# Mixture-of-experts blocks that scatter their rows into token order, instead of a gather afterwards

## The reference

```python
# e0: 8 experts, hidden 704; e1: 7 experts, hidden 256, plus a shared expert; e3: 8 experts, hidden 512
probs = router(x)                       # softmax, or sigmoid in e1
w, idx = top_k(probs, 2); w = w / sum(w)
for each token t and k in (0, 1):
    e = idx[t, k]
    y[t] += w[t, k] * (silu(x[t] @ gate[e]) * (x[t] @ up[e])) @ down[e]
```

## Time and profile before

| | |
|---|---|
| span of the profiled execution | 2167.4 us |
| median of three runs | 2168.05 us |
| TensorE busy | 1686.6 us (78%) |
| VectorE busy | 1150.7 us (53%) |
| ScalarE busy | 544.3 us (25%) |
| GpSimd busy | 544.7 us (25%) |
| HBM read / written | 231.86 MB / 30.02 MB |
| mean granted TensorE clock | 0.891 of full speed |

### The profile page before, as it was taken

One profiled execution on the slowest core, in us unless ns is written; L12 is line 12 of the kernel. 1 busy time (PEld: TensorE's weight loads), 2 busy tenths in 40 slices (PEclk: granted clock), 3 DMA queues, 4 the chain that ended last, 5 costly groups with the idle time before them and its releaser, 6 DMA issues. The chain is left out here.

```text
span 2167.4 us, 36689 instructions
## 1 busy us (share of the span) xinstructions
PE 1686.6 (78%) x10302; PEld 1354.6 (62%) x10302; DVE 1150.7 (53%) x2756; ACT 544.3 (25%) x1372; POOL 544.7 (25%) x812
## 2 busy tenths in 40 slices
PE   3994999997269787999994878716799599499990
PEld 2772889886169644666663467605566487398980
DVE  5774222221966667777767223365788577422223
ACT  1441011010134223556551110002222254110100
POOL 1001111111510014666652033250122100222215
PEclk8996999999589888999997899955899799699995
DMA  3103889986200026535301078830000000399983
GB/s 111 35 0 114 293 295 304 299 288 222 75 1 0 0 73 121 74 42 73 43 1 39 15 236 267 250 94 1 0 0 0 1 0 0 127 324 313 322 272 119
DMA packets 182133, 262.59 MB, mean 121 GB/s; under 512 B 17504, under 2 KB 132640, under 8 KB 180032
## 3 DMA queue, kind: packets, MB, share of 16 engines
q1 hardware_dynamic: 171856, 234.01, 36.2%
q0 software_dynamic: 10224, 27.93, 4.8%
HBM read 231.86 MB, written 30.02 MB: 121 GB/s over the span
## 5 line engine op out<-in xcount | busy, mean ns | idle before, releaser
L992 POOL TENSOR_TENSOR l1a_pr<-l1a_pr,l1a_rc (+4 forms) x256 | 176.0, 719 | 113.5 <-DVE l1a_rc L932 113.4
L956 ACT ACTIVATE l1a_pr<-l1a_sc,l1a_nm 128x256 f32 (+7 forms) x256 | 131.4, 525 | 113.3 <-DVE l1a_nm L926 113.3
L1049 PE MATMUL l1a_ob<-l1a_pT,xn 128*128 128x512 f32 (+3 forms) x512 | 148.5, 434 | 0.0
L1049 PEld LDWEIGHTS l1a_ob<-l1a_pT,xn 128*128 128x128 f32 x512 | 92.3, 191 | 50.9 <-issue 30.6
L1578 PEld LDWEIGHTS e0b_gp<-e0b_xT,e0b_wgu 128*128 128x128 f32 x936 | 109.4, 195 | 14.7 <-issue 12.3
L1162 POOL DMA_INDIRECT e_got<-y_slots,e_slot x96 | 99.8, 1040 | 73.7 <-issue 71.4
L1578 PE MATMUL e0b_gp<-e0b_xT,e0b_wgu 128*128 128x128 f32 x936 | 116.9, 283 | 1.8 <-DVE e0b_hT L1647 1.3
L1599 PE MATMUL e0b_yp<-e0b_wd,e0b_hT 128*128 128x256 f32 x468 | 115.2, 388 | 0.6 <-issue 0.6
L926 DVE TENSOR_REDUCE l1a_nm<-l1a_sc 128x1 f32<-128x512 f32 (+3 forms) x256 | 107.2, 482 | 0.2 <-PE l1a_sc L1027 0.2
L1628 ACT ACTIVATE e0b_sg<-e0b_gp 128x640 f32<-128x640 f32 x78 | 33.5, 481 | 288.0 <-PE e0b_gp L1578 288.0
L519 PE MATMUL a_sc<-a_kd,a_qT 128*128 (+2 forms) x256 | 99.4, 523 | 4.4 <-ACT a_qT L592 2.9
(11 more groups left out here) (475 smaller groups left out, 3581.3 us busy)
## 6 DMA issues: line engine op xcount, KB each, us to landing
e3b_wgu<-in_L_ffn_W SPq DMA_DIRECT2D x78, 512.0 KB, 5.6
e0b_wgu<-in_L_ffn_gate_proj SPq DMA_DIRECT2D x39, 704.0 KB, 4.6
e0b_wgu<-in_L_ffn_up_proj SPq DMA_DIRECT2D x39, 704.0 KB, 6.0
e0b_wd<-in_L_ffn_down_proj SPq DMA_DIRECT2D x39, 640.0 KB, 5.2
e3b_wd<-in_L_ffn_W SPq DMA_DIRECT2D x39, 512.0 KB, 6.4
e1b_wgu<-in_L_ffn_Wg_r SPq DMA_DIRECT2D x39, 256.0 KB, 3.8
e1b_wgu<-in_L_ffn_Wu_r SPq DMA_DIRECT2D x39, 256.0 KB, 4.5
e1b_wd<-in_L_ffn_Wd_r SPq DMA_DIRECT2D x39, 256.0 KB, 4.0
```

What stands on the lines that cost most here:

```text
L956: nc.scalar.activation(pr[:, n & 1, of_query[q]], sc[q][:, 0:(q + 1) * P], ACT.Exp, bias=nm[:, q:q + 1], accum_out=sums[:, n & 1, q:q + 1] ...
L992: nc.gpsimd.tensor_tensor(of, of, bcast(rc[:, n & 1, q:q + 1], 2, (q + 1) * P), ALU.mult)\
L1049: last = nc.tensor.matmul(ob[:, k * P:], vz[:, k, h * P:(h + 1) * P], pT[:, n & 1, key_at[k]:key_at[k] + TB - k, :], start=(h == 0 and k = ...
```

## The change

- The blocks' results are no longer stored by SP. POOL stores them: `send(n, j)` waits until `copy_out(n)` is done, copies a column of the new table `target` into `row`, waits for it, runs a filler and issues an indirect DMA (a scatter) from `yb` into `y_rows`, whose row number is 256 + 2048 k + token. Places without a token write into the first 256 rows. `send(n)` stands at the end of POOL's `step(n)`, behind the fetch of block n+3 and in front of the `step(n+1)` that fetches block n+4.
- `route` makes `target` beside `token`: seven VectorE instructions at its end instead of three. Two constants grow or are added.
- In the combination, POOL issues nothing more. SP issues eight plain loads of four token tiles each (128 x 4 rows of 1 KB, 512 KB), alternately for k = 0 and 1, into a ring of four. Load n of 4 or later waits until the tiles of load n-4 are used. In e0 and e1 they stand behind `beside.load` in SP's queue.

```diff
+    y_rows = nc.dram_tensor("y_rows", [2 * P + TOP * B * S, D], F32, kind="Internal").ap()
+    RING, RING_TILES = 4, 4
...
-                        for n in range(T * TOP):
-                            if n >= RING:
-                                pool.wait_ge(used, n - RING + 1)
-                            pool.indirect_dma_start(got[:, n % RING, :], None, y_slots[0:NB * P, :], bass.IndirectOffsetOnAxis(
-                                ap=slot[n % TOP][:, n // TOP:n // TOP + 1], axis=0)).then_inc(rows_got[n % RING], 16)
...
+                        for n in range(LOADS):
+                            if n >= RING:
+                                sp.wait_ge(used, (n - RING) // TOP * TOP * RING_TILES + (RING_TILES - 1) * TOP + n % TOP + 1)
+                            c, k = n // TOP, n % TOP
+                            sp.dma_start(got[:, n % RING, :, :], by_token[k, :, c * RING_TILES:(c + 1) * RING_TILES, :])\
+                                .then_inc(rows_got[n % RING], 16)
...
-                    nc.vector.tensor_copy(token_p[:], found[:, 1, :]).then_inc(step, 1)
+                    nc.vector.tensor_scalar(token_p[:], found[:, 1, :], float(B * S - 2 * P), None, ALU.add).then_inc(step, 1)
+                    nc.vector.scalar_tensor_tensor(spare_row[:], found[:, 0, :], 0.0, const("spare"), ALU.is_equal, ALU.mult)\
+                        .then_inc(step, 1)
...
-                    dve.wait_ge(step, 32)
-                    nc.vector.tensor_copy(token[:], token_f[:])
+                    dve.wait_ge(step, 33)
+                    nc.vector.tensor_copy(token_i[:], token_f[:]).then_inc(step, 1)
+                    nc.vector.scalar_tensor_tensor(target_f[:], token_f[:], float(2 * P - B * S), spare_row[:], ALU.add, ALU.add)\
+                        .then_inc(step, 1)
+                    dve.wait_ge(step, 34)
+                    nc.vector.tensor_scalar(token[:], token_i[:], B * S - 1, None, ALU.bitwise_and)
+                    dve.wait_ge(step, 35)
+                    nc.vector.tensor_copy(target[:], target_f[:])
...
-                        if positive(n):
-                            store(n - 1, 1 - j)
-
-                    def store(n, j):
-                        sp.wait_ge(y_copied, n + 2)
-                        sp.dma_start(y_slots.rearrange("(n p) d -> n p d", p=P)[n], yb[j][:]).then_inc(rows_out[j], 16)
...
+                    def send(n, j):
+                        pool.wait_ge(y_copied, n + 2)
+                        nc.gpsimd.tensor_copy(row[j][:], target[:, bass.ds(n, 1)]).then_inc(row_ready, 1)
+                        pool.wait_ge(row_ready, n + 1)
+                        nc.gpsimd.tensor_tensor(spare[:], const("place"), const("place"), ALU.add)
+                        pool.indirect_dma_start(y_rows, bass.IndirectOffsetOnAxis(ap=row[j][:], axis=0), yb[j][:], None)\
+                            .then_inc(rows_out[j], 16)
...
                         fetch(1 - j)
+                        send(n, j)
...
+                    send(0, 0)
                     with pool.Fori(0, (NB - 5) // 2) as i:
                         for j in (1, 0):
                             step(i * 2 + 2 - j, j)
                     step(NB - 4, 1)
+                    for n in (NB - 3, NB - 2, NB - 1):
+                        send(n, n % 2)
```

More of the change, by code:

```diff
@@ L61, in _constants @@
         "iota128": np.tile(np.arange(P), (P, 1)),
-        "tiles": np.tile(np.arange(T), (P, 1)),
+        "tiles": np.tile(np.arange(TOP * T) + 2, (P, 1)),
+        "spare": p[:, None] + P * (np.arange(ROUTED)[None, :] % 2),
         "place": p[:, None],
@@ L142, in build @@
     x_rows = nc.dram_tensor("x_rows", [B * S, D], F32, kind="Internal").ap()
-    y_slots = nc.dram_tensor("y_slots", [SLOTS, D], F32, kind="Internal").ap()
-    RING = 16
+    y_rows = nc.dram_tensor("y_rows", [2 * P + TOP * B * S, D], F32, kind="Internal").ap()
+    RING, RING_TILES = 4, 4
     pool_sem = lambda n: ctx.enter_context(nc.semaphore(n))
@@ L1128, in experts @@
             token = tmp("token", [P, ROUTED], U32)
+            target = tmp("target", [P, ROUTED], U32)
             with ExitStack() as s2:
@@ L1131, in experts @@
                 normalise(f"{tag}n", x, xn, rms_weight, (lp, wr, E), st6)
-                route(tag, lp, E, wt, slot, owner, token, bias, x, outer)
+                route(tag, lp, E, wt, slot, owner, token, target, bias, x, outer)
             if shared:
                 shared_expert(f"{tag}s", *shared, F, into)
-            blocks(tag, w_gate, w_up, w_down, F, NB, E, owner, token)
+            blocks(tag, w_gate, w_up, w_down, F, NB, E, owner, token, target)
             with ExitStack() as s2:
                 sem = Semaphores(nc, s2, tag)
-                got = s2.enter_context(nc.sbuf_tensor(f"{tag}_got", [P, RING, D], F32))
+                got = s2.enter_context(nc.sbuf_tensor(f"{tag}_got", [P, RING, RING_TILES, D], F32))
                 used = sem("used")
+                LOADS = T * TOP // RING_TILES
+                by_token = y_rows[2 * P:].rearrange("(k t p) d -> k p t d", k=TOP, p=P)
                 if beside is not None:
@@ L1175, in _ @@
                                 beside.round(dve, n // 8)
-                            dve.wait_ge(rows_got[n % RING], 16 * (layer * T * TOP // RING + n // RING + 1))
+                            load = t // RING_TILES * TOP + k
+                            dve.wait_ge(rows_got[load % RING], 16 * (layer * LOADS // RING + load // RING + 1))
                             if n:
                                 dve.wait_ge(used, n)
-                            nc.vector.scalar_tensor_tensor(into[:, t, :], got[:, n % RING, :], wt[k][:, t:t + 1], into[:, t, :],
-                                                           ALU.mult, ALU.add).then_inc(used, 1)
+                            nc.vector.scalar_tensor_tensor(into[:, t, :], got[:, load % RING, t % RING_TILES, :], wt[k][:, t:t + 1],
+                                                           into[:, t, :], ALU.mult, ALU.add).then_inc(used, 1)
                             if k == TOP - 1 and t:
@@ L1274, in _, with route @@
                     add(B - 1)
-    def route(tag, lp, E, wt, slot, owner, token, bias, x, outer):
+    def route(tag, lp, E, wt, slot, owner, token, target, bias, x, outer):
         NB = ROUTED
@@ L1302, in route @@
             token_p, token_f = tmp("token_p", [P, ROUTED]), tmp("token_f", [P, ROUTED])
+            token_i, spare_row, target_f = tmp("token_i", [P, ROUTED], U32), tmp("spare_row", [P, ROUTED]), tmp("target_f", [P, ROUTED])
             found = ps("found", [P, 2, ROUTED])
@@ L1337, in _ @@
                     for k in range(TOP):
-                        nc.gpsimd.tensor_tensor(numbers[k][:, :, 0, :], at_hot[k][:], bcast(const("tiles"), 2, ROUTED), ALU.mult)\
+                        nc.gpsimd.tensor_tensor(numbers[k][:, :, 0, :], at_hot[k][:],
+                                                bcast(const("tiles")[:, k * T:(k + 1) * T], 2, ROUTED), ALU.mult)\
                             .then_inc(hot, 1)
@@ L1446, in _, with blocks @@
                         .then_inc(step, 1)
-                    dve.wait_ge(step, 32)
-                    nc.vector.tensor_copy(token[:], token_f[:])
-    def blocks(tag, w_gate, w_up, w_down, F, NB, experts_n, owner, token):
+                    dve.wait_ge(step, 33)
[6 more added lines that the diff above has]
+                    nc.vector.tensor_copy(target[:], target_f[:])
+    def blocks(tag, w_gate, w_up, w_down, F, NB, experts_n, owner, token, target):
         assert F % P in (0, P // 2)
@@ L1477, in blocks @@
             index = [st.enter_context(nc.sbuf_tensor(f"{tag}b_index{j}", [P, 1], U32)) for j in range(2)]
+            row = [st.enter_context(nc.sbuf_tensor(f"{tag}b_row{j}", [P, 1], U32)) for j in range(2)]
             spare = tmp("spare", [P, 1])
-            index_ready = sem("index")
+            index_ready, row_ready = sem("index"), sem("row")
             gu_in, d_in = ([sem(f"{n}{j}") for j in range(2)] for n in ("guin", "din"))
@@ L1531, in _ @@
                     step(NB - 2, 1, gate_up=False)
-                    for n in (NB - 2, NB - 1):
-                        store(n, n % 2)
                     sp.wait_ge(rows_out[0], 16 * (before[0] + NB // 2 + 1))
```

## The result

The kernel after takes 2222.09 us (median, 2220.1 to 2226.64), the kernel before 2168.41 us on the same chip: a ratio of 1.0244, 95% interval 1.0224 to 1.0265. It is slower, and by more than was forecast: the median lies 43 us above the 2179, and 15 us above the upper end of the range. The profiled execution has a span of 2219.1 us, 51.7 more than before, and a mean granted TensorE clock of 0.881 (before 0.891).

The account below looks back on a forecast made before the run. Bound: e3's combination by POOL's gathers, the blocks by TensorE, in e1 partly by weight loads. Combination -22.2, route +2.1, POOL's order +19.4 in e1 and +11.8 in e3 sum to +11.1 us on 2168.05: 2179, range 2155 to 2207.

Parts of the forecast that it names:

- The loop: Blocks: copy-out, send, fetch, landing, turn, up, down, copy-out over two blocks; costs +19.4 us in e1, +11.8 in e3, 0 in e0.
- first piece: Blocks, from the copy's end to the fetch's DMA: notice 0.17, send 0.75 + 0.99, index copy 0.75, together 2.66 us.
- The landing L in e1: Time from the fetch's DMA start to its landing in e1's blocks: between 2.9 and 4.4 us, taken as 3.4.
- The upper bound: e1's blocks: landing of 4.4 us, giving 4.93 us a block, +1.06, and up to +37 us.
- the last piece, turn to copy: Blocks, from the turn's start to the copy's end: 2.69 us in e1, 4.45 in e3.
- 5.45 + L: Length of e1's closed loop over two blocks, L being the fetch's landing; with 3.4 it is 8.85 us, 4.43 a block.
- The way out of the blocks: Each stage's end, last copy to SP's next load: notice and issue 0.92, landing 2.9, then 0.37: 4.2 us against 2.1.
- Combination and route: Combination: e3 -16.5, e1 -7.8, e0 +2.1, together -22.2 us; route: four more VectorE instructions a stage, +2.1 us for three.
- The fast landing: Rival, blocks: stall thins out the traffic, fetches land fast; e1 costs 11 us, e3 little or nothing; 2159, chance 0.25.
- the queue behind the send: Rival, blocks: fetch queues behind the send in the one software queue, landing 5.6 in e3, 4.4 in e1; 2209, chance 0.13.
- The case that the eight loads don't keep up: Rival, combination: a pair lands after 7.5 us instead of 4.9, the ring stalls twice a stage; +12 us, 2191, chance 0.07.
- list of signs: Periods 4.4 in e1, 6.0 in e3; some 35 turns wait; index copy follows send; e3's combination about 29 us, additions 0.655 apart.

Follow-up runs that it names:

- e0: Not a run: one of the kernel's three expert stages, hidden size 704; its block period is 7.99 us in both the kernel before and after.
- e3: Not a run: the expert stage that ends last, hidden size 512; its block period is 5.74 us in the kernel before, 5.97 after.
- fetch_first: Kernel after, with POOL's send of block n-1 behind the fetch of block n+3, one block later than in the change: 2159.68 us, ratio to before 0.9931.
- wait_and_filler: Kernel before with SP's stores; POOL's step also waits for the same copy-out, copies a column and runs a 1.04 us filler, no scatter: 2217.11 us.
- last_by_sp: Kernel after, but SP stores blocks 37 and 38 of each stage with plain DMAs to the spare rows: 2202.57 us, ratio to before 1.0146.
- half_weights: Kernel after, but e1's gate and up loads bring half of their bytes from block 2 on: 2199.69 us.
- merged: fetch_first with the combination in the expert blocks' block of programs, no barrier between, matrices loaded ahead of SP's wait: 2125.86 us, ratio to before 0.9792.

## Why the prediction was wrong, and where it was right

The direction and the mechanism were right, and two terms of the sum were too small: e1's blocks by 31 us and the ways out of the blocks by 12. Both errors point the same way, and together they carry the result out of the range.

*The loop.* It exists as described: its first piece was forecast at 2.66 and is 2.62, e3's period at 6.06 and is 5.97 (pieces 2.55, 4.91 and 4.48 us), e0's loss at nothing and it is nothing. For e1, fetch_first and wait_and_filler show it from both sides. For e3 only fetch_first does: with the loop opened e3's loss is gone, but wait_and_filler, whose loop is 0.55 us shorter, shows no loss there. (The base of 3.87 us a block was read off the stores; the copies give 3.92, which changes little.)

*The landing L in e1.* The step that failed is "L falls as the stall grows; I take 3.4". I had taken it for a function of the average DMA share. The share fell indeed, further than thought (0.65), and still fetch to turn is 4.28 us over the turns that waited, where the forecast had 3.5. These traces say that what is issued beside the fetch counts more. In the iteration shown above SP's loads of gate and up (1353.80 and 1354.37) are issued right ahead of the fetch at 1354.71, whose turn waits. The next fetch, at 1357.96, comes 3.6 us behind them and 3.5 ahead of the next two, and its turn doesn't wait. The trace of after has no landings of the indirect DMAs. That of last_by_sp has them, with the same blocks up to 36: 4.1 us on average for the fetches whose turn waits, 2.9 for the others. half_weights shows that the bytes of those loads cost 0.9 us. The upper bound, the measured median of 4.4, was the better value.

*TensorE's clock.* Missing from the sum altogether, and the larger of the two errors. I carried the last piece, turn to copy, over from the trace of before at 2.69, where TensorE had no long idle time and a clock of 0.98. The added stall was taken as spread over all blocks, half a microsecond each. It comes bunched instead: 18 waits of 3.0 us, one for every two blocks, and behind 15 of them the piece takes over 3.3 us, up to 4.67, with the granted clock at its lower level for a part or all of it. The step is the last term of "5.45 + L": 4.06 behind a turn that waited, instead of 2.69, and 2.76 behind one that didn't. Of the 2.00 us by which the waiting loop is longer than forecast (10.85 for 8.85), 1.37 are this piece and 0.78 the landing, while the first piece gives 0.15 back. By a rule in the Trainium skill ("TensorE: Matmul & The Clock Gate", section "HAM oscillation — how this bites in real kernels"), a kernel whose short stretches of matmuls alternate with waits for DMA is thrown back to the half clock over and over. This case's trace agrees: 0.82 in e1, and 0.98 again with dummy work in the waits. The two errors feed each other, since a longer wait lets the clock fall and the slower products lengthen the loop: a block takes 5.25 us with both, 4.64 with TensorE kept busy, 4.57 with half of the gate and up traffic; the forecast, with neither, was 4.43. Why the waits pair up isn't settled; POOL issues send, fetch, send, fetch in a row behind one copy-out (1353.07 to 1357.96), which would do it.

*The way out of the blocks.* The step that failed is "Sum 0.92 + 2.9 + 0.37 = 4.2". The landing in it was fine, even a little high: merged measures 3.14 from the last copy to the first load. But the 0.37 came from a stage whose last instructions were SP's stores, while POOL had issued its last indirect DMA 14 us earlier. What isn't in that row is POOL's drain ahead of the barrier, 6.44 us from the end of its last indirect DMA. 0.67 to the scatter, 1.00 for it, 6.44, and 0.24 to the load make 8.35. That is 4.15 us more than forecast at each stage's end, which is most of the miss in e3 (-11.9 for -16.5) and e1 (-3.7 for -7.8), and nearly that in e0.

*Combination and route.* Right: 4.0 and 5.5 us from the first load's issue to the first and the second addition (forecast 3.6 and 4.9), then 1.31 us a pair with no stall of the ring, so eight loads do keep up. The rest is +2.1, as forecast for route; how much of it is route's wasn't separated.

*The rivals.* The fast landing is refuted by L, the queue behind the send by wait_and_filler for e1, and for e3 by the landings, which stay at a median of 4.9 to 5.1 us with and without scatters, where this rival had 5.6. The case that the eight loads don't keep up is refuted by the additions' pace. None of them had the clock or the drain. The forecast's list of signs held in its kind (turns that wait, the index copy behind the send, faster additions) but not in number: in e1 18 waits behind the first turn instead of some 35, in e3 14. A send takes 1.02 us at most in all three stages, so the row of the blocks was the right one for it. The rule of the Trainium skill weighed there ("DMA: Bandwidth & Descriptors", section "SWDGE vs HWDGE vs iDMA") would have made it 2.4, and the trace doesn't bear that out in the blocks.

## What to carry to other kernels

When an instruction with a wait is put into the queue of an engine that prefetches, follow the prefetched data to its consumer: if the awaited result comes behind that consumer, a closed loop has arisen, and putting the waiting instruction one block later opens it (here at no cost in either stage). Price such a loop with the measured median of a transfer and with the clock that TensorE gets behind waits of that length, not with the busy stretch of the kernel before. And read its pieces over the turns that really waited: an average over all of them mixes a landing with the lateness of a consumer whose data lie ready. And an indirect DMA just ahead of a barrier costs POOL's drain; do without the barrier, or have the last results stored by another engine.

## What the runs showed of the hardware that I had not expected

- POOL's drain at the end of a block of programs ended 6.44 us behind the end of its last scatter (15 stage ends in five kernels, all within 0.01) and 4.3 to 4.5 us behind that of a gather, though the scatter's landing was noticed 2.5 us after its issue. In e3 nothing else was running then. What the drain waits for isn't shown.
- Idle time of TensorE costs twice: e1's 54 us of waits for rows behind the first turn came with some 24 us more of matmul time for the same work (132.89 against 109.23), and keeping TensorE busy with ten useless 128x128 transposes a block took 23 us off the stage.
- A scatter of 128 rows of 1 KB takes POOL 1.0 us, like a gather (0.99), and lands after 2.4 us at best.
- Two fetches of 128 rows each, mostly some 3 us apart in the same queue, land after 4.1 and 2.9 us on average (last_by_sp, e1): the first comes right behind SP's loads of gate and up, the second between two pairs of them. The average DMA share (0.64 in that stretch) doesn't show this.
